# Stores of the q and k parts issued by ScalarE instead of SyncE in an attention and expert layer

## The reference

```python
h = tok(x)                                    # (8, 744, 256): three shifted frames by W, + b
h = h + attn(layernorm(h))                    # 16 heads of 16, causal softmax
h = h + ffn(layernorm(h))                     # 4 experts of width 1024, the best 2 for each row

k, q, v = heads(x @ Wk.T), heads(x @ Wq.T), heads(x @ Wv.T)
att = softmax(where(causal, q @ k.T / 4, -inf))
y = (att @ v) @ Wp.T + bp
```

## Time and profile before

| what | value |
|---|---|
| median of 3 runs | 1739.21 us (1738.99 to 1742.22) |
| profiled execution | 1728.33 us |
| its span, first to last instruction | 1726.6 us |
| mean granted TensorE clock | 0.937 |
| busy: PE, DVE, ACT, POOL | 1523.0, 1101.6, 707.3, 836.9 us |
| stores of q and k parts | 64 of 279.0 KB |
| store of h1, of the residual result | 8 of 755.6 KB, 8 of 744.0 KB |

### The profile page before, as it was taken

One profiled execution on the slowest core, in us unless ns is written; L12 is line 12 of the kernel. 1 busy time (PEld: TensorE's weight loads), 2 busy tenths in 40 slices (PEclk: granted clock), 3 DMA queues, 4 the chain that ended last, 5 costly groups with the idle time before them and its releaser, 6 DMA issues.

```text
span 1726.6 us, 33232 instructions
## 1 busy us (share of the span) xinstructions
PE 1523.0 (88%) x10648; PEld 1185.3 (69%) x10648; DVE 1101.6 (64%) x3477; ACT 707.3 (41%) x1464; POOL 836.9 (48%) x912
## 2 busy tenths in 40 slices
PE   6598898997988988988978777899999999999997
PEld 5364474564564654744745434889999999999997
DVE  3367777677687787687776650755555555555554
ACT  1135644634545545445445443233333333333332
POOL 5315435635536546447356342165564544444445
PEclk9689998999999998999999877999999999999998
DMA  3623635635536536436436764265645546455451
GB/s 109 149 55 98 153 101 146 150 94 164 143 90 181 129 104 174 122 111 179 116 110 167 216 217 146 76 201 183 210 166 185 197 154 208 170 171 189 165 200 38
DMA packets 166972, 256.24 MB, mean 148 GB/s; under 512 B 30484, under 2 KB 97998, under 8 KB 166800
## 3 DMA queue, kind: packets, MB, share of 16 engines
q1 hardware_dynamic: 108816, 166.66, 33.0%
q10 hardware_dynamic: 34368, 50.33, 9.1%
q0 software_dynamic: 23616, 37.12, 7.6%
HBM read 173.92 MB, written 75.29 MB: 144 GB/s over the span
## 4 chain that ended last, share of the span: by engine, by line
PE 51%; DVE 13%; issue 12%; DMA 10%; SPq 5%; POOL 4%; ACT 3%; ACTq 0%; DVEq 0%; POOLq 0%
PE yb L1521 14%; PE l1b L1505 13%; PE pab L1341 8%; PE pvb L1453 5%; PE mxb L1409 4%; PE stb L1428 4%; DVE unused L1040 4%; DMA qk_s<-parts 3%; DMA qst<-negp 3%; SPq L593 2%; POOL xs L698 2%; DVE mxp L1043 2%; SPq L561 1%; PE rb L1470 1%; ACT hf L943 1%
## 5 line engine op out<-in xcount | busy, mean ns | idle before, releaser
L857 ACT ACTIVATE prob<-stb 124x496 f32<-124x496 f32 (+2 forms) x832 | 398.0, 505 | 407.8 <-PE stb L1428 378.4
L1040 DVE CUSTOM_DVE_ANT_0 unused<-mxb,mask_row 124x372 bf16<-124x372 f32 (+4 forms) x768 | 352.2, 484 | 72.7 <-PE mxb L1409 68.9
L1409 PE MATMUL mxb<-kst,qst 96*124 96x372 bf16 (+4 forms) x1024 | 315.9, 341 | 84.4 <-DVE mxp L1040 52.9
L1428 PE MATMUL stb<-qst,kst 99*124 99x372 bf16 (+4 forms) x1024 | 310.1, 336 | 40.9 <-ACT prob L857 19.1
L1521 PE MATMUL yb<-w2p,hp 128*128 x2448 | 335.3, 282 | 12.1 <-DVE yo L1296 11.7
L1505 PE MATMUL l1b<-x2T,w1s 128*128 128x384 f32 x1632 | 339.9, 344 | 1.2 <-DVE x2T L1250 1.2
L1521 PEld LDWEIGHTS yb<-w2p,hp 128*128 128x128 f32 x2448 | 320.8, 189 | 22.6 <-issue 22.6
L943 ACT ACTIVATE hf<-l1b,b1c 128x384 f32<-128x384 f32 x272 | 158.3, 582 | 350.2 <-PE l1b L1505 307.2
L1505 PEld LDWEIGHTS l1b<-x2T,w1s 128*128 128x128 f32 x1632 | 277.9, 190 | 1.5 <-DVE x2T L1250 1.4
L1409 PEld LDWEIGHTS mxb<-kst,qst 96*124 96x124 bf16 x1024 | 138.7, 144 | 175.0 <-DVE mxp L1040 94.7
L1282 DVE CAST hp<-hf 128x384 fp32r<-128x384 f32 x272 | 105.3, 387 | 236.4 <-ACT hf L943 189.5
(11 more groups left out here) (178 smaller groups left out, 1492.9 us busy)
## 6 DMA issues: line engine op xcount, KB each, us to landing
w1s<-ws SPq DMA_DIRECT2D x34, 2048.0 KB
qk_s<-parts SPq DMA_DIRECT2D x64, 279.0 KB
xg<-xs SPq DMA_DIRECT2D x34, 396.0 KB
kst<-qk_s SPq DMA_DIRECT2D x32, 279.0 KB, 3.7
qst<-qk_s SPq DMA_DIRECT2D x32, 279.0 KB, 5.2
wraw<-in_w_all ACTq DMA_DIRECT2D x32, 256.0 KB
ws<-whi ACTq DMA_DIRECT2D x32, 256.0 KB
ws<-wlo ACTq DMA_DIRECT2D x32, 256.0 KB
```

Source lines behind the costliest of these rows:

```text
L857: act.activation(dst, src, ACT.Exp, scale=DH ** -0.5).then_inc(exp_done, 1)
L1040: done = dve.tensor_tensor_reduce(out=unused[:, n % 2, e * w:(e + 1) * w], in0=src, in1=mask_row[:, T - w:T], scale=1.0, scalar=-3.0e38, o ...
L1409: done = nc.tensor.matmul(out, qst[g % NG][0:ROWS, h + e, TT * i:TT * i + TT], kst[g % NG][0:ROWS, h + e, k0:k0 + w], start=True, stop=True)
L1428: done = nc.tensor.matmul(out, kst[g][:, h, TT * j:TT * j + TT], qst[g][:, h, q0:q0 + w], start=True, stop=True)
```

## The change

A new kind of event, `qk_store`, stands two slots behind each `qk` (in the front: after the next `qk`). ScalarE issues the store there, after a wait for `qk_low`; SyncE no longer does. The new kind is among those that `bank_in_turn` holds. The loads of the stacks, the folds and the negated maxima remain with SyncE. Transfers, sizes, buffers and all else are as before.

```diff
@@ front_events
     for n in range(8):
         yield "qk", n
+        if n:
+            yield "qk_store", n - 1
+        if n == 7:
+            yield "qk_store", n
@@ body_events
         for n in range(4):
             put(38 + 3 * n, "qk", n)
+            put(40 + 3 * n, "qk_store", n)
             put(59 + 3 * n, "qk", n + 4)
+            put(61 + 3 * n, "qk_store", n + 4)
@@ bank_in_turn
-        if turning and e[0] in ("v", "proj", "tok", "turn", "qk", "h1_store", "load_stack", "h2_store",
+        if turning and e[0] in ("v", "proj", "tok", "turn", "qk", "qk_store", "h1_store", "load_stack", "h2_store",
@@ SyncE, emit
-                    if kind == "qk":
-                        sp.wait_ge(qk_low, a * 8 + n + 1)
-                        sp.dma_start(qk_s[a, n // 2 % 2, n // 4, :, :, :, n % 2 * HALF:(n % 2 + 1) * HALF]
-                                     .rearrange("t r h c -> (r h) t c"),
-                                     parts[:, (a * 8 + n) % PB, :, :]).then_inc(parts_stored[(a * 8 + n) % PB], 16)
@@ ScalarE, emit
+                    if kind == "qk_store":
+                        act.wait_ge(qk_low, a * 8 + n + 1)
+                        act.dma_start(qk_s[a, n // 2 % 2, n // 4, :, :, :, n % 2 * HALF:(n % 2 + 1) * HALF]
+                                      .rearrange("t r h c -> (r h) t c"),
+                                      parts[:, (a * 8 + n) % PB, :, :]).then_inc(parts_stored[(a * 8 + n) % PB], 16)
```

## The result

The changed kernel takes 1754.67 us (median of 5 runs, 1749.07 to 1758.15), the kernel before 1738.99 on the same chip: ratio 1.0095, with a 95% interval of 1.0068 to 1.0123. It is slower by 15.7 us. Among the later experiments it was timed again, with 1.0082 (1.0053 to 1.0111).

A forecast was written before the change was run, and what follows sets the result against it. TensorE was busy 88% of the span, with neither transfers nor ScalarE the bound on average, yet ScalarE's stops could hold the rest. Terms +7.8, +3.6, +2.5, -3.5 and -1.5 gave +8.9 us on 1739.2: 1748 us, range 1728 to 1768.

The forecast's parts named there:

- the forecast case: Whole kernel: ScalarE's late exponentials and evacuations make it slower, 1743 to 1765 us; chance 0.55.
- Bound and mechanism: Bodies: ScalarE, though much idle, can hold the other engines if it stops for two slots.
- The wait: ScalarE before each of 56 body stores: 1.1 to 2.3 us for GpSimd's third part, none free.
- A long issue: ScalarE's queue: an issue costs 1.3 us with two transfers unfinished, 0.4 with fewer; pieces 2, 3, 5, 6 candidates.
- Stage A: Slots 38 to 52, six bodies: late evacuation of piece 3 delays slot 52 by 1.3 us each, +7.8 us.
- Stage B: Slots 59 to 78, six bodies: evacuations 5 to 7 pushed, partly covered; +0.6 us each, +3.6 us.
- stack 0: Bodies: piece 3's store no longer behind folds, so TensorE's stack waits shrink; -3.5 us, between 0 and -10.1.
- Negated maxima: Stage A: the move could save 1.0 us per body, but that is lost behind VectorE; counted as nothing.
- First body and front: First body: uncovered slots 38 to 52 delay, +2.5 us; front: stack 0 load sooner, -1.5 us.
- Rival 1, relief wins: Whole kernel faster: stacks and maxima arrive sooner, ScalarE's idle time swallows the waits; 1727 us, chance 0.22.
- Rival 2, nothing: Whole kernel same: waits fall where `st` waits for maxima anyway, small gains pay the rest; 1739 us, chance 0.16.
- Rival 3, the ring backs up: Slower: four issues per body behind two unfinished transfers wait 3 us, not 1.3; 1768 us, chance 0.07.

The follow-up runs named there:

- the kernel that only waits: Kernel before, SyncE still storing, with ScalarE only waiting for the third part two slots behind each product in the bodies: 0.9985, 1734.91 us.
- wait alone: Kernel before with residual store in slot 36, plus ScalarE only waiting for the third part, SyncE still storing: 0.9949, 1730.94 us.
- issue alone: Changed kernel with ScalarE's stores four slots behind each product and the residual store in slot 36: 0.9938, 1729.53 us.
- stores four behind: Changed kernel with each body store four slots behind its product instead of two, residual store still in slot 42: 1.0116, 1759.56 us.
- residual store late: Changed kernel with the residual store in slot 50 instead of 42, behind the store of piece 3: 1.0218, 1778.96 us.

## Why the prediction was right in sign and range and wrong in its terms

The sum of +8.9 us forecast the sign and 1748 us; measured were +15.7 and 1754.7, inside the range and inside the own range of the forecast case. The terms are less good than their sum. In the profiles the stages add up to +25.6 us, nearly three times the forecast: one large cost was missed, and a cost and a gain further on were both under-sized and nearly cancel. That the medians lie closer to the forecast than the profiles do is luck.

- **Bound and mechanism: right.** A stop of ScalarE, idle for more than half of the span, held the other engines. Slot 52 is released by VectorE and no longer by the maxima, as stated. The evacuation of piece 3 begins 4.45 us after that of piece 2 (median of the six bodies; 3.08 before), as "4 us or more" said.
- **The wait: there, and free by itself in the first kernel that tried it.** ScalarE waits 1.2 to 1.8 us for the third part of pieces 0 to 6, and for that of piece 7 only 0.6 us in six of seven bodies, where 1 us or more was forecast for all. Issue included it is held 1.1 to 2.5 us (forecast 1.6 to 2.8), except 4.2 to 4.6 at the six held issues and 3.9 at one piece 7. The step "none of them free" failed as a cost: with the residual store in its place the kernel that only waits has 0.9985. With that store early the same wait took 3.4 to 7.9 us, which may be noise. Where the loss can be placed, something else stands in the same place: a held issue, or three issues in a row.
- **A long issue: the right mechanism in the wrong place and size.** The argument rested on the store of the residual result being followed by a load at 0.34 us, and concluded that one unfinished transfer costs nothing. But that load came 6.0 us behind it. The store of piece 1 comes 2.9 us behind and takes 2.5 to 2.8 us. Pieces 2, 3, 5 and 6 were named as candidates; all their issues are under 0.5 us. The estimate of 9 us for the residual store itself was good (it moves for 9.3 us, the last byte 10.1 us behind the issue), but it is not what counts: the hold ends some 4 us before the store does. The price of 1.3 us for a long issue stood in place of 2.5 to 2.8, and piece 1 was given +0.2 us where the interval from its evacuation to that of piece 2 grew from 4.33 to 6.75.
- **Stage A: +7.8 forecast, +22.4 in the profiles,** outside the +2.4 to +13.2 that the prediction gave it. 18.1 of it goes when the residual store is moved, most of that the hold. The rest is what wait and short issues cost: 4.3 us against before, 6.4 against before with its residual store early as well. That is less than forecast.
- **Stage B and stack 0: +3.6 and -3.5 forecast.** Slots 52 to 66 lose 15.4 us and slots 66 to 78 win 13.2, together +2.2 against +0.1. The push at piece 4 was priced well: 1.7 to 2.7 us for the evacuation of piece 5, and the interval from piece 4 to piece 5 grew by 2.0 (3.02 to 4.98). What was mis-sized is how much of it stays: +0.6 us in a body after covers, where slots 52 to 66 lose 2.1 us in a body by TensorE's starts (2.6 by the exponentials). The covers came, but only behind slot 66, and pieces 5 and 6 did not repeat the push (5 to 6: 3.51 to 3.44). The gain was under-sized as well: stack waits went from 10.1 and 14.8 us to nothing where the forecast left room for "under 6", and 66 to 70 alone is 10 us shorter (6 by TensorE's starts).
- **Negated maxima: counted as nothing, not nothing.** The waits of `st` on them in TensorE's weight loads fall from 19.3 (21.1) to 9.2 us. At slot 52 this is mostly TensorE coming later, since they land only 0.4 us faster there (6.1 to 5.7 us at the mean). Slots 70 to 78 shrink from 55.2 to 52.1 us (58.6 to 53.7 by TensorE's starts), so they may have given 3 to 5 us there.
- **First body and front: near the forecast**, about +2 (2.5) and -1 (-1.5), but the two profiles of before differ by 2.9 and 1.9 us there, so this confirms little.
- **Rival 1, relief wins,** had the relief right (slots 66 to 78) and missed that it is paid for. Its deciding point, evacuation 3 slipping by less than 1.0 us, was passed: it slips 1.4 against piece 2, which itself slips 2.4. **Rival 2, nothing,** is out by the interval (1.0068 to 1.0123). **Rival 3, the ring backs up,** was right that an issue can cost 3 us, and wrong in needing two unfinished transfers and four such issues in a body; one unfinished long store was enough, once per body.

The Trainium skill ("DMA: Bandwidth & Descriptors", section "Issuing engines are not separate DMA queues") says that issuing from several engines saves only the time of the issue, and calls that time usually small beside the transfer. Here the time of the issue is small at 58 of 64 stores (0.38 us of 3.8 to landing at the median), and not small right behind the residual store: up to 5.48 us. And more than the issue changed with the queue. In the same page's section "Queues, rings and completion order" stands the rule that the prediction weighed, that a ring is served in order and rings take turns, and the traces agree with it. Landings are recorded for one slot of `parts` in three. In the changed kernel (minimum, median, maximum):

```profile
DMA to landing us min/median/max: 2.9/3.8/10.2
```

The two stores of piece 1 among them, behind the residual store in the same ring, land 9.9 and 10.2 us after their issue began. Issued by SyncE beside the same residual store they take 7.5 to 8.6 us (six bodies of the kernel that only waits), and with the residual store early 3.0 to 4.1 us from ScalarE's ring. The engine that issues suffered as well, and that is what TensorE felt: stack 0, which needs these parts, was not waited for.

**What stays open.** The profiles put before some 24 us ahead of the changed kernel, the medians 14 to 16; the shares above are those of profiles. With the residual store early, wait alone and issue alone took 2 to 8 us more and both together 11 to 16, so it is not settled how much of the 0.7% is the two meeting; a part of it is placed (slots 62 to 66), and not proved by a kernel that takes it away. Why before gains 13 to 17 us by the early store is argued from its waits. And what makes the hold, and what of the two transfers sets its length, is open: splitting or reshaping the residual store was not tried.

**The best kernel** is the one before with the residual store in slot 36: 0.9903 and 0.9926, 1723.05 and 1727.55 us. It beats both kernels, and it leaves the stores with SyncE. The kernels that add to it only the wait, or the stores four slots behind, took 2 to 8 us more, which is near the noise. It is one number in the order of work, and it was found by asking what the long transfer stands in the way of.

## What to carry to other kernels

An issue that takes 0.3 us somewhere in the trace says nothing of one that comes sooner behind a long transfer: look at how long ago the last large transfer of the same queue was issued, and keep any issue on a computing engine clear of that time. A stop on an engine with slack may be made up for when it stands alone and be paid when others stand right behind it, so price what stands in one place between two evacuations, and not a kind of operation by its count. And before moving transfers to another engine, try moving the one large transfer that they collide with.

## What the runs showed of the hardware

A store of a q or k piece that came within 3 us behind the issue of the residual store (744.0 KB) was not accepted by ScalarE's queue until 5.5 to 5.8 us after that issue, and the later it came in that time, the shorter its own issue. Start of the next issue behind that store, its duration, and both together:

| where (six bodies each) | behind, us | issue, us | end, us |
|---|---|---|---|
| stores four behind, piece 0 | 0.33 | 5.2 to 5.5 | 5.5 to 5.8 |
| changed kernel, piece 1 | 2.9 to 3.0 | 2.5 to 2.8 | 5.5 to 5.8 |
| residual store late, h1 store (755.6 KB) | 2.9 to 3.4 | 3.4 to 5.3 | 6.7 to 8.5 |
| before, weight load (one of them in the earlier trace rows) | 6.0 | 0.34 | 6.4 |
| changed, residual store early, piece 0 | 6.6 to 8.8 | 0.38 (0.94 once, at 6.6) | 7.5 to 9.2 |

So the end of the hold is no constant of the first store alone. The h1 store was held longer, and a piece's store at 6.6 us was still held a little where a weight load at 6.0 was not; that the kind of the next transfer makes the difference is likely and was not tested. When the hold ended at 5.5 to 5.8 us, about half of the residual store had been moved. The hold stops the instructions of ScalarE that are written behind it, not only its transfers, and it does not show as busy time of the engine (702.4 us against 707.3). A weight load 0.5 us behind a piece's store and 7.9 us behind the residual store cost 1.3 to 2.0 us (six bodies of the kernel with piece 1 on SyncE). The second surprise was that a long store in ScalarE's queue delays transfers in SyncE's. The negated maxima (5.8 KB each) of group 2 took 5.4 to 6.5 us to land in before and 2.0 to 2.5 with the residual store six slots earlier. The store of piece 1 by SyncE took 7.5 to 8.6 us beside the residual store and 3.2 in the first body, which has none. The 10 to 15 us of waits for stacks in before went to 1 us by the same move, with nothing changed in SyncE's order.
